# A state-space recurrence with its squares and end scaling on ScalarE, the first-decay product formed ahead of the norm, output sums by segment, and inputs spread over three segments

## The reference, cut to what matters

```
A    = -exp(soft_clamp(A_log, -5, 5, 0.5))
dt_A = soft_clamp(dt[..., None] * A, -8, 8, 0.5)     # soft_clamp is a scaled tanh
dA   = exp(dt_A)
for t in range(512):                                  # h: [batch, 256, 16]
    h   = h * dA[t] + dt[t] * B[t] * x[t]
    fac = min(20 / (sqrt(sum(h * h)) + 1e-8), 1)      # one norm per sequence
    if t % 10 == 0: h = h * fac
    y[t] = sum over n of h * C[t, n]  +  D * x[t]
x_ssm = y * silu(gate)
```

## Time and profile before

| | |
|---|---|
| median of 3 runs | 6191.43 us |
| lowest and highest | 6186.78 and 6191.97 us |
| the profiled execution, its own time | 6185.92 us |
| its span, first to last instruction | 6184.0 us |
| mean granted TensorE clock over the span | 0.867 |
| PE, VectorE (DVE), ScalarE (ACT), GpSimd (POOL) busy over the span | 81%, 52%, 48%, 31% |
| the recurrence, from its first matmul to its last | 4094.8 to 4633.9 us |

### The profile page before, as it was taken

The page is one execution under the profiler, slowest core; times in us unless marked ns, Lnnn a source line. Parts: engine busy times, 40 slices in busy tenths (PEclk is TensorE's granted clock), DMA queues, the critical chain, the costliest instruction groups (busy, mean ns, idle before and its releaser), DMA issues. The chain is left out here.

```text
span 6184.0 us, 108311 instructions
## 1 busy us (share of the span) xinstructions
PE 5032.6 (81%) x39346; PEld 3240.5 (52%) x39346; DVE 3189.3 (52%) x6332; ACT 2957.8 (48%) x8829; POOL 1901.8 (31%) x2082
## 2 busy tenths in 40 slices
PE   3998598978878878878788788778989944787888
PEld 2664255756636546546456456458886632223433
DVE  5551354556546446455356366358875544562433
ACT  2442244547647657556467477355534412352421
POOL 0230000347637457367277187001112300000000
PEclk6999799999989989899899799776669966895888
DMA  1000000001101111111111011000000000000000
GB/s 48 2 1 4 19 10 16 1 14 39 47 19 41 40 29 36 35 34 35 31 39 41 25 40 41 32 1 1 1 1 5 1 3 4 10 4 29 4 0 7
DMA packets 34520, 122.70 MB, mean 20 GB/s; under 512 B 8484, under 2 KB 9512, under 8 KB 32424
## 3 DMA queue, kind: packets, MB, share of 16 engines
q1 hardware_dynamic: 33960, 115.42, 6.9%
HBM read 36.43 MB, written 1.05 MB: 6 GB/s over the span
## 5 line engine op out<-in xcount | busy, mean ns | idle before, releaser
L640 POOL MEMSET norm_eps<- 128x1 f32 x16 | 1.6, 99 | 1905.7 <-POOLq L116 1847.2
L2087 POOL TENSOR_TENSOR local_rot<-local_raw,local_cos 128x512 f32<-128x512 f32 x384 | 488.1, 1271 | 303.5 <-DVE local_raw L2131 303.5
L2090 POOL TENSOR_TENSOR local_other<-local_raw,local_sin 128x256 f32<-128x256 f32 x768 | 557.6, 726 | 60.2
L2029 ACT ACTIVATE ps<-ps,local_negmax 128x96 f32<-128x96 f32 x1536 | 489.2, 322 | 37.2 <-DVE local_negmax L2110 36.9
L1952 PE MATMUL ps<-arena,local_xs 128*128 128x512 f32 x768 | 447.4, 667 | 71.8 <-ACT local_xs L2009 52.0
L2093 POOL TENSOR_TENSOR local_rot<-local_rot,local_other 128x512 f32<-128x512 f32 x384 | 487.4, 1269 | 30.1
L2024 ACT ACTIVATE local_squares<-ps 128x512 f32<-128x512 f32 x384 | 230.8, 601 | 508.2 <-PE ps L1952 507.8
L2117 DVE TENSOR_REDUCE local_norm<-local_squares 128x8 f32<-128x512 f32 x384 | 263.2, 685 | 282.4 <-ACT local_squares L2024 282.4
L1940 PE MATMUL ps<-local_K,local_Q 64*64 64x96 f32 x6144 | 337.0, 249 | 0.0
L2029 ACT ACTIVATION_READ_ACCUMULATOR ps<-ps,local_negmax 128x1 f32 x1536 | 331.0, 215 | 0.0
L2519 PE MATMUL ps<-ssm_BC,const 32*128 32x40 f32 (+1 forms) x3584 | 297.8, 373 | 26.4 <-PEq L116 22.0
(11 more groups left out here) (499 smaller groups left out, 11465.9 us busy)
## 6 DMA issues: line engine op xcount, KB each, us to landing
local_V_span<-local_V SPq DMA_DIRECT2D x96, 384.0 KB, 4.0
local_V_span<-local_V SPq DMA_DIRECT2D x96, 256.0 KB, 3.5
arena<-in_L1f_a SPq DMA_DIRECT2D x7, 2176.0 KB, 8.2
local_V_span<-local_V SPq DMA_DIRECT2D x72, 128.0 KB, 2.3
arena<-in_L3f SPq DMA_DIRECT2D x1, 3460.0 KB, 11.6
arena<-in_L1f_f SPq DMA_DIRECT2D x6, 537.5 KB, 4.0
arena<-in_L0f SPq DMA_DIRECT2D x1, 2824.5 KB, 9.8
arena<-in_L0x SPq DMA_DIRECT2D x1, 2049.5 KB, 9.0
```

The costliest lines, as they stand in the source:

```text
L2029: nc.scalar.activation(scores, scores, ACT.Exp, bias=m.negmax[:, s % 2, u:u + 1], accum_out=m.total[:, s % 2, u:u + 1])\
L2087: link(nc.gpsimd.tensor_tensor(rot, raw, m.cos[:, t, a * DH:(a + 1) * DH].unsqueeze(1) .broadcast_to([P, 8, DH]), ALU.mult))
L2090: link(nc.gpsimd.tensor_tensor(other[:, :, lo:lo + HALF], raw[:, :, HALF - lo:DH - lo], m.sin[:, t, a * DH + lo:a * DH + lo + HALF].unsque ...
```

## The change

- The squares move from VectorE (L2631) to ScalarE (an activation with Square).
- The end states are scaled by ScalarE: one instruction per sequence, 4 per segment, in place of VectorE's L2653.
- VectorE multiplies the unscaled end states by the next first decay into a new buffer `pre` before it waits for the norm, and afterwards forms scratch = pre * fac.
- The decays of a chunk are cut into four quarters, each with its own 8 Tanh, Exp, copy and zeroing, and spread over the segments of the chunk before.
- The output sums are made per segment: 32 identity matmuls of 40 columns in every segment (16 for each half), one segment behind, in place of 32 of 160 columns per chunk. D times x is added at i = 1 in place of i = 2.
- The B takes are spread 4, 6, 6 over segments 1, 2 and 3 in place of 8 and 8 over segments 2 and 3, and the spreads are spread over all four segments.
- At i = 0 only the first half of the weighing stands before the norm's reduce, the second half behind it.

```diff
+        return [(kind, k + 1, h, p) for kind, h, p in
+                {0: [("B", 0, 0), ("B", 0, 1)], 1: [("B", 1, 0), ("C", 0, 0)], 2: [("B", 1, 1)],
+                 3: [("C", 0, 1), ("C", 1, 0), ("C", 1, 1)]}[i]]
...
+    TAKES = 0, 4, 6, 6
...
+        def before(k, i):
+
+            if i > 0:
+                return (k, i - 1) if exists(k) and i < segs_of[k] else (-1, 0)
+            return (k - 1, segs_of[k - 1] - 1) if exists(k - 1) else (-1, 0)
...
-                    if exists(k - 1) and i < 2:
-                        if i == 0:
-                            pe.wait_ge(weighed, 2 * segs_before[k])
-                            if k >= 2:
-                                pe.wait_ge(y_read, 2 * (k - 1))
-                        for n in range(SSM_N):
-                            mm = nc.tensor.matmul(y_rows(k - 1, i), core.ident,
-                                                  H[:, (k - 1) % 2, 0:segs_of[k - 1], :, i * SSM_N + n, :]
-                                                  .rearrange("p s b t -> p b s t"),
-                                                  start=(n == 0), stop=(n == SSM_N - 1))
-                        mm.then_inc(y_ready, 1)
+                    kk, ii = before(k, i)
+                    r = segment(kk, ii)
+                    if r is not None:
+                        pe.wait_ge(weighed, 2 * (r + 1))
+                        if ii == 0 and kk >= 1:
+                            pe.wait_ge(y_read, 2 * kk)
+                        for c in range(2):
+                            for n in range(SSM_N):
+                                mm = nc.tensor.matmul(y_rows(kk, c)[:, :, ii * SEG:(ii + 1) * SEG], core.ident,
+                                                      H[:, kk % 2, ii, :, c * SSM_N + n, :],
+                                                      start=(n == 0), stop=(n == SSM_N - 1))
+                            mm.then_inc(y_ready, 1)
...
+                for i in range(4):
+                    s = segment(k, i)
+                    if s is not None:
+                        act.wait_ge(scanned, s + 1)
+                        nc.scalar.activation(sq[:, :, :], ends(k, i), ACT.Square, scale=1.0 / LIMIT).then_inc(sq_ready, 1)
...
+                    early = QUARTER // 2 if i == 0 and k >= 0 else QUARTER
+                    for j, q in decays(k, i):
+                        rates_of(j, q, range(QUARTER * q, QUARTER * q + early))
+                    if s is not None:
+                        act.wait_ge(fac_ready, s + 1)
+                        for b in range(B):
+                            nc.scalar.mul(ends(k, i)[:, b, :], ends(k, i)[:, b, :], fac[:, b:b + 1]).then_inc(scaled, 1)
+                    for j, q in decays(k, i):
+                        rates_of(j, q, range(QUARTER * q + early, QUARTER * (q + 1)))
+                        decays_of(j, q)
...
-                        nc.vector.scalar_tensor_tensor(out=sq[:, :, :], in0=ends(k, i), scalar=LIMIT ** -2,
-                                                       in1=ends(k, i), op0=ALU.mult, op1=ALU.mult).then_inc(sq_ready, 1)
...
+                            link(nc.vector.tensor_tensor(pre[:, :, :], first[:, nk % 2, ni, :, :], ends(k, i), ALU.mult))
...
-                        last = nc.vector.tensor_tensor(ends(k, i), ends(k, i),
-                                                       fac[:, :].unsqueeze(2).broadcast_to([P, B, DN]), ALU.mult)
...
+                            link(nc.vector.tensor_tensor(scratch[:, :, :], pre[:, :, :], fac[:, :].unsqueeze(2)
+                                                         .broadcast_to([P, B, DN]), ALU.mult))
```

More of the change, by code:

```diff
@@ L2414, in state_recurrence @@
     u = buf("u", [P, 2, B, 2, SSM_CHUNK])
-    sq, scratch = buf("sq", [P, B, DN]), buf("scratch", [P, B, DN])
+    sq, scratch, pre = buf("sq", [P, B, DN]), buf("scratch", [P, B, DN]), buf("pre", [P, B, DN])
     half = buf("half", [P, B])
@@ L2453, in spreading, with copying, taking_of, decays @@
             return []
-        return {1: [("B", k + 1, 0, 0), ("B", k + 1, 0, 1)], 2: [("B", k + 1, 1, 0), ("B", k + 1, 1, 1)],
-                3: [("C", k + 1, h, p) for h in range(2) for p in range(2)]}.get(i, [])
+        return [(kind, k + 1, h, p) for kind, h, p in
+                {0: [("B", 0, 0), ("B", 0, 1)], 1: [("B", 1, 0), ("C", 0, 0)], 2: [("B", 1, 1)],
+                 3: [("C", 0, 1), ("C", 1, 0), ("C", 1, 1)]}[i]]
+    def copying(k, i):
+        return [use for use in spreading(k, 1) if use[0] == "C"] if i == 2 else spreading(k - 1, 3) if i == 0 else []
+    TAKES = 0, 4, 6, 6
+    def taking_of(k, i):
+        if not exists(k + 1):
+            return []
+        all_of = [(use, c, b) for i in range(4) for use in spreading(k, i) if use[0] == "B"
+                  for c in range(2) for b in range(2)]
+        lo = sum(TAKES[:i])
+        return all_of[lo:lo + TAKES[i]]
+    QUARTER = DN // 4
+    def decays(k, i):
+        units = [(k + 2, 0)] if i == 3 else [(k + 1, i + 1)]
+        if k == -1 and i == 0:
+            units = [(0, 0)] + units
+        return [u for u in units if exists(u[0])]
     def place(use):
@@ L2525, in _ @@
         def _(act):
-            for k in CHUNKS_ALL:
[L2527 to L2553, removed]
@@ new lines, in rates_of @@
+            def rates_of(j, q, ms):
+                if q == 0 and j >= 2 and 0 in ms:
+                    act.wait_ge(scanned, segs_before[j - 1])
+                cols = slice(SSM_CHUNK * j, SSM_CHUNK * j + length(j))
+                for m in ms:
+                    nc.scalar.activation(dA[j % 2][:, 0:segs_of[j], :, m, :].rearrange("p s b t -> p b s t"),
+                                         by_segment(dt[:, :, m // SSM_N, cols]), ACT.Tanh, scale=rate[:, m:m + 1])\
+                      .then_inc(tanh_ready, 1)
@@ L2584, in _, with weigh @@
             link = Chain(dve, step)
-            def weigh(k, i):
+            def weigh(k, i, c):
                 s = segment(k, i)
-                if i == 0:
+                if s is None:
+                    return
+                if i == 0 and c == 0:
                     dve.wait_ge(copied, 4 * (k + 1))
[L2591 to L2617, removed]
@@ new lines, in weigh, with take @@
+                dve.wait_ge(scaled, B * (s + 1))
+                part = H[:, k % 2, i, :, c * SSM_N:(c + 1) * SSM_N, :]
+                nc.vector.tensor_tensor(part, part, C_rows[k % 2][:, :, :, i * SEG:(i + 1) * SEG], ALU.mult)\
+                  .then_inc(weighed, 1)
+            def take(use, c, b):
+                kind, j, h, p = use
+                dve.wait_ge(spread["B"], place(use) + 1)
+                if h == 0 and p == 0:
+                    dve.wait_ge(u_ready, j + 1)
+                    if j >= 2:
+                        dve.wait_ge(y_ready, 2 * segs_before[j - 1])
+                lo = c * SSM_N + HALF * h
+                nc.vector.tensor_tensor(H[:, j % 2, 0:segs_of[j], 2 * p + b, lo:lo + HALF, :]
+                                        .rearrange("p s n t -> p n s t"),
+                                        u[:, j % 2, 2 * p + b, c, 0:length(j)].unsqueeze(1)
+                                        .broadcast_to([P, HALF, length(j)]).rearrange("p n (s t) -> p n s t", t=SEG),
+                                        rows(use)[:, b, :, :].rearrange("p n (s t) -> p n s t", t=SEG),
+                                        ALU.mult).then_inc(taken, 1)
@@ L2643, in _ @@
                                                            op0=ALU.mult, op1=ALU.add).then_inc(y_read, 1)
[L2644 to L2648, removed]
+                    for use, c, b in taking_of(k, i):
+                        take(use, c, b)
                     if s is not None:
```

62 lines of the change are left out of this document (41 added, 21 removed).

## The result

The changed kernel takes 6792.55 us (median of 4, 6789.12 to 6798.66) against 6189.1 us for the kernel before on the same chip: a ratio of 1.0977, interval 1.0964 to 1.0990. Forecast were 6768 us, and a range of 6660 to 6830.

A forecast was written before the change was run, and what follows sets the result against it. VectorE was taken to set the pace before, PE at clock 0.50 after: sums 722, spreads 303, norms 32 and new waits 36 make 1093 us against 517, plus 1.5, so +577 and 6768 us; range 6660 to 6830.

The forecast's parts named there:

- The clock: PE's granted clock, 0.65 before, stays at 0.50 for the whole recurrence, as the 160-column sums seen to raise it go.
- Sums: Output sums on PE: 3392 passes of 40 columns at 0.213 us, 722 us, low bound 673.
- Spreads: Spreads on PE after the first norm: 3328 passes at 0.091 us, 303 us, bounds 283 and 323.
- New waits: PE idles twice per chunk, at i = 0 and i = 1, for VectorE: 36 us, bounds 0 and 52.
- Norms: Norm matmuls on PE, two passes in each of 53 segments at 0.6 us: 32 us, at most 42.
- Sum: PE's time from its first norm, output sums, spreads, norms and waits together: 1093 us, against 517 before.
- VectorE and ScalarE at nothing: VectorE's 22 us less work and ScalarE's new squares and scaling cost 0, hidden behind PE's sums.
- the signs forecast: Expected in the changed profile: VectorE waits longest for the norm's matmul, 8 to 12 us a segment; ScalarE's scan wait similar.
- Rival C: The sums fit under VectorE, which saves work and half its norm and root waits: -51 us, 6140 us, chance 0.02.
- VectorE sets the pace: In the kernel before, VectorE bounds the recurrence and PE follows with about a tenth to spare.
- A: The main case: PE bounds the recurrence at clock 0.50, 6768 us, between 6663 and 6841, chance 0.86.

## Why the prediction was right

- **The clock.** Right: 0.50 over the whole recurrence. The page "TensorE: Matmul & The Clock Gate" of the Trainium skill, Part 1, has sustained activity release the throttle; here PE is busy for 97% of 1136 us at 0.50, so this trace does not agree for matmuls of 40 columns. The extra wide matmuls showed the reason from the other side: the clock rises in their block and falls in the 40-column work behind it.
- **Sums.** Forecast 722 us, measured 730.7 of PE's time, 0.213 us a pass from start to start (13.65 us for 64). The one block of 40-column sums in the trace of before carried the whole forecast.
- **Spreads.** Mis-sized: forecast 303 us after the first norm. A chunk now has groups of 3.64, 6.23, 7.05 and 8.82 us, 25.7 us, and 13 of them 334. A use costs 2.6 us and each group about 1.05 more for its start. The group of 7.05 has 0.82 on top: there, by the code's order, B(1, 0) is followed by C(0, 0), and both read the same 64 partitions (p = 0), where elsewhere p changes from use to use. The 256 passes at the start fit this, though no run isolates it: 21.79 us before, eight uses and one start, and 23.43 now, with two such places. The term took 0.091 us a pass on average and had too little for four starts; its high bound, 323, was too low as well.
- **New waits.** Forecast 36 us, measured 31.6, at the two places and with the two causes named: 1.18 us for the weighing, 1.12 for D times x.
- **Norms.** 32 forecast, at most 42; 0.58 us to the next start where the sums follow at once and 0.80 in the 26 segments with a new wait, 37.
- **Sum.** From the first norm to the last reading of the sums 1093 forecast, 4116.30 to 5243.90 is 1127.6: 35 us more, nearly all of it the spreads. The median was missed by 25 only, and that is luck: 5.5 us were added since the median before lay above the profiled execution, and now it lies 1.1 below; the 1.5 us ahead of the first norm did not come, and the program outside the recurrence took some 2 us less.
- **VectorE and ScalarE at nothing.** Right in this kernel: VectorE's work fell from 439 to 410 us, 29 less where 22 were forecast, and it shows nowhere. Of the signs forecast, VectorE's wait for the norm came out at 12.9 us per segment against 8 to 12. ScalarE was put wrong: it waits 354 us for `fac` and 376 for spreads, and 23.8 for the scan.
- **Rival C** had a price of -51 us if the sums had fitted. The experiments refute that price: with the sums by chunk the rest of the change made the recurrence 14.6 us longer, because PE held two of four steps in a chunk, and of the other two one gave back what the other gained. It held them before the change too, so "VectorE sets the pace" in the prediction's first paragraph is true of the other two steps only; no term of A rests on it. Half of VectorE's waits, which the price counted as filled, were not: its wait for the norm grew from 27.0 to 76.4 us:

```profile
L2693 DVE TENSOR_REDUCE ssm_sums<-ps 128x4 f32<-128x128 f32 x53 | 15.4, 291 | 76.9 <-PE ps L2522 76.4
```

What stays open: why a pass of 40 and one of 80 columns cost the same 0.21 us at the lower clock. The kernels here show that it is so, not what the time is spent on. The weight loads keep pace with the passes (PEld is busy for 1086 us of the 1136), but no run leaves them out, so that the load is the cost is argued, not shown.

## What to carry over

Cutting a matmul group in four costs four times its passes, and here, at the lower clock, a pass of 40 columns cost 0.21 us where one of 160 cost 0.26: before splitting work by time, count passes on the engine that is nearly full, and price them from a row of the new shape, which may exist in a remainder block at the end. Ask as well during which instructions the clock is seen to rise, since removing them reprices everything else on that engine. And with two engines near full, look step by step at which one comes late before relieving the other.

## What was not expected

- 32 passes of 80 columns took 6.95 us, 64 of 40 took 13.71 us.
- Sixteen extra matmuls per segment (394.8 us of PE) cut the sums' own time by 214 us: the same passes, at a clock that is partly up.
- A GpSimd operation on 128x4 took 1.52 us beside a VectorE multiplication of 128x640 and 1.01 us otherwise.
- A sublayer that nobody touched ran at clock 1.00 or 0.50 from one kernel to another, 55 us apart.
